# Full attention: small jobs on turned maxima and outputs moved from VectorE to ScalarE and GpSimd

## The reference

```python
def _L1_attn_ref(x, Wq, bq, Wk, bk, Wv, bv, Wo, bo):
    q = (x @ Wq.T + bq).reshape(b, s, NHEADS, DK)
    k = (x @ Wk.T + bk).reshape(b, s, NHEADS, DK)
    v = (x @ Wv.T + bv).reshape(b, s, NHEADS, DV)
    w = jnp.einsum('bshd,bzhd->bhsz', q, k)
    w = w / jnp.sqrt(jnp.float32(DV))
    w = jax.nn.softmax(w, axis=-1)
    vw = jnp.einsum('bhsz,bzhd->bshd', w, v)
    out = vw.reshape(b, s, NHEADS * DV) @ Wo.T + bo
    return out
```

## Time and profile before

| what | us |
|---|---|
| median of three runs (2055.39 to 2059.88) | 2056.86 |
| span of the profiled execution | 2056.4 |
| attention stage, first exponential to last division | 986.4 to 1637.7 |
| of it, first to last exponential, 256 steps | 986.4 to 1634.0 |
| busy in the whole span: PE / DVE / ACT / POOL | 1579.5 / 1339.0 / 1135.7 / 550.2 |

### The profile page before, as it was taken

One profiled execution on the slowest core, in us unless ns is written; L12 is line 12 of the kernel. 1 busy time (PEld: TensorE's weight loads), 2 busy tenths in 40 slices (PEclk: granted clock), 3 DMA queues, 4 the chain that ended last, 5 costly groups with the idle time before them and its releaser, 6 DMA issues. The chain is left out here.

```text
span 2056.4 us, 34421 instructions
## 1 busy us (share of the span) xinstructions
PE 1579.5 (77%) x11512; PEld 917.7 (45%) x11512; DVE 1339.0 (65%) x3318; ACT 1135.7 (55%) x2965; POOL 550.2 (27%) x615
## 2 busy tenths in 40 slices
PE   6799999999991699245999999999999735424910
PEld 3478777777771699221222222222222234323910
DVE  5655656656564322267999999999999287842523
ACT  3366766666651344142688888888888733111300
POOL 2133323524526400571001001001000020372056
PEclk9799999999995799666899999999999967556965
DMA  5144311211101676142000000000000000013832
GB/s 191 39 156 156 107 30 36 54 28 43 42 21 37 203 234 205 52 122 83 23 21 26 18 26 18 27 18 26 19 25 2 1 0 6 21 45 124 253 91 72
DMA packets 86203, 138.99 MB, mean 68 GB/s; under 512 B 18084, under 2 KB 57252, under 8 KB 85900
## 3 DMA queue, kind: packets, MB, share of 16 engines
q1 hardware_dynamic: 62860, 92.08, 15.2%
q0 software_dynamic: 11936, 34.49, 5.1%
q10 hardware_dynamic: 11232, 10.23, 1.4%
HBM read 75.51 MB, written 45.11 MB: 59 GB/s over the span
## 5 line engine op out<-in xcount | busy, mean ns | idle before, releaser
L2062 DVE TENSOR_REDUCE q_max<-s_ps 128x1 f32<-128x1024 f32 x512 | 598.2, 1219 | 14.0 <-PE s_ps L1953 6.8
L2043 ACT ACTIVATE probs<-s_ps 128x512 f32<-128x512 f32 x1024 | 535.5, 603 | 124.5 <-PE s_ps L1974 124.3
L1953 PE MATMUL s_ps<-k_stack,q_stack 64*128 64x512 bf16 x1024 | 351.2, 397 | 16.9 <-PEq L96 8.5
L1974 PE MATMUL s_ps<-q_stack,k_stack 64*128 64x512 bf16 x1024 | 319.5, 384 | 20.2 <-ACT probs L2043 15.8
L1988 PE MATMUL o_ps<-probs,v_aug 128*32 128x512 f32 x2048 | 273.6, 606 | 0.7 <-ACT probs L2043 0.7
L1974 PEld LDWEIGHTS s_ps<-q_stack,k_stack 64*128 64x128 bf16 x1024 | 78.6, 94 | 333.9 <-ACT probs L2043 281.9
L989 POOL TENSOR_TENSOR probs<-probs,p_rsum 128x512 f32<-128x512 f32 x128 | 132.9, 1038 | 325.8 <-DVE p_rsum L966 325.1
L869 ACT ACTIVATE probs<-s_biased,s_min 128x128 f32<-128x128 f32 (+1 forms) x512 | 197.7, 391 | 37.0 <-DVE s_min L960 35.6
L734 PE MATMUL score_ps<-k_pad,q_bd 128*128 128x128 f32 x1024 | 146.7, 287 | 0.0
L960 DVE CUSTOM_DVE_ANT_0 s_biased<-score_ps,nbias 128x128 f32<-128x128 f32 (+1 forms) x512 | 115.8, 282 | 41.8 <-PE score_ps L734 40.6
L1580 POOL CAST neg_max_parts<-neg_max 16x128 bf16<-16x128 f32 x32 | 9.0, 281 | 474.7 <-DVE neg_max L2070 474.7
(11 more groups left out here) (315 smaller groups left out, 2824.5 us busy)
## 6 DMA issues: line engine op xcount, KB each, us to landing
moe0b_wblock<-in_L_ffn_blocks SPq DMA_DIRECT2D x39, 578.0 KB, 3.9
moe_rows<-zero_rows POOLq DMA_DIRECT2D x18, 960.0 KB, 4.4
moe1b_wblock<-in_L_ffn_blocks SPq DMA_DIRECT2D x39, 256.0 KB, 3.5
v_shift<-v_tiles SPq DMA_DIRECT2D x32, 256.0 KB, 3.1
v_shift<-v_tiles SPq DMA_DIRECT2D x32, 224.0 KB, 3.6
qk_parts_dram<-qk_parts SPq DMA_DIRECT2D x16, 384.0 KB, 2.7
q_stack<-qk_parts_dram SPq DMA_DIRECT2D x192, 32.0 KB
k_stack<-qk_parts_dram SPq DMA_DIRECT2D x192, 32.0 KB
```

Of the source, the lines that this page charges most:

```text
L1953: mm = nc.tensor.matmul(s1[u % 2][:, c * CH:(c + 1) * CH], qs[head_rows(m), quad % 4, j, qt * P:(qt + 1) * P], ks[head_rows(m), quad % 4, ...
L1974: nc.tensor.matmul(bank_of("exp", 4 * k + pos)[:], ks[head_rows(m), quad % 4, j, kt * P:(kt + 1) * P], qs[head_rows(m), quad % 4, j, half ...
L2043: nc.scalar.activation(pr[:, k % 2, HEADS[pos], :], bank_of("exp", n)[:], ACT.Exp).then_inc(sm["exp"], 1)
L2062: v.tensor_reduce(mx[:, h % 4, col:col + 1], s1[u % 2][:], AX.X, ALU.max).then_inc(sm["maxed"], 1)
```

## The change

Three things are moved; TensorE's program keeps its order, and waits for the new release of a bank (`o_read` in place of `o_done`).

- The negation of the turned maxima goes from VectorE to ScalarE, as an activation Copy with scale -1.
- The turned outputs, 9 columns of 16 head and token groups, are copied by ScalarE from the bank into a new tile `o_tokens` in two buffers; that copy frees the bank.
- GpSimd divides from `o_tokens`: a power with the exponent -1 on the sums, then the product into `nat`. It sets a tile of -1 once ahead of the loop.

VectorE keeps the row maxima alone. ScalarE does the moved work of step k - 1 behind the first exponential of step k. The core of the diff:

```diff
             @block.gpsimd
+                def divide(m):
+                    pool.wait_ge(sm["o_read"], m + 1)
+                    if m >= 2:
+                        pool.wait_ge(sm["o_done"], m - 1)
+                    nc.gpsimd.tensor_tensor(ro[:, m % 2], ot[:, m % 2, :, :, HD1], minus[:], ALU.pow).then_inc(sm["o_rsum"], 1)
+                    pool.wait_ge(sm["o_rsum"], m + 1)
+                    nc.gpsimd.tensor_tensor(
+                        K.nat[:, t:t + CPT, s * 32:(s + 1) * 32].rearrange("p t (h d) -> p t h d", d=HD1),
+                        ot[:, m % 2, :, :, 0:HD1], bc(ro[:, m % 2], 3, HD1), ALU.mult
+                    ).then_inc(sm["o_done"], 1)
...
                 for quad in range(NQ):
                     if quad >= 2:
+                        divide(2 * quad - 3)
                         pool.wait_ge(sm["pv_mm"], STEPS * (quad - 1))
...
                     if quad >= 1:
                         split_max(2 * quad - 1)
+                        divide(2 * quad - 2)
                     split_max(2 * quad)
+                divide(2 * NQ - 3)
                 split_max(2 * NQ - 1)
+                divide(2 * NQ - 2)
+                divide(2 * NQ - 1)
...
             @block.scalar
+                def negate_max(h):
+                    act.wait_ge(sm["m_turned"], h + 1)
+                    if h >= 1:
+                        act.wait_ge(sm["m_split"], 4 * h)
+                    nc.scalar.activation(nm[:], turned_view(bank_of("m_neg", h))[0:HU, 0, :], ACT.Copy, scale=-1.0
+                                         ).then_inc(sm["m_neg"], 1)
+                def read_output(m):
+                    act.wait_ge(sm["o_turned"], m + 1)
+                    if m >= 2:
+                        act.wait_ge(sm["o_done"], m - 1)
+                    heads = turned_view(bank_of("o_read", m)).rearrange("p t (h c) -> p t h c", c=32)
+                    nc.scalar.copy(ot[:, m % 2], heads[:, :, :, 0:HD1 + 1]).then_inc(sm["o_read"], 1)
+                def behind_first(k):
+                    if max_done_at(k) is not None:
+                        negate_max(max_done_at(k))
+                    if output_due_at(k) is not None:
+                        read_output(output_due_at(k))
+                negate_max(0)
                 for k in range(NK):
                     for pos in range(4):
...
+                        if pos == 0 and k >= 1:
+                            behind_first(k - 1)
                         if pos == 2 and k % TPB == 0 and k >= TPB:
                             output(k // TPB - 1)
+                behind_first(NK - 1)
                 output(2 * NQ - 1)
+                read_output(2 * NQ - 1)
...
             @block.vector
-                    if u == HU:
-                        negate_max(0)
                 for k in range(NK):
                     for u in step_units(k):
                         reduce_max(u)
-                    if max_done_at(k) is not None:
-                        negate_max(max_done_at(k))
-                    if output_due_at(k) is not None:
-                        divide(output_due_at(k))
-                divide(2 * NQ - 1)
```

More of the change, by code:

```diff
@@ L1765 @@
             "m_stored", "m_loaded",
-            "s2_mm", "exp", "v_aug", "pv_mm", "o_out", "o_turned", "o_done", "o_rsum")
+            "s2_mm", "exp", "v_aug", "pv_mm", "o_out", "o_turned", "o_read", "o_rsum", "o_done",
+            "minus_set")
 def full_attention_stage(nc, K, A, wo, M):
@@ L1827, in full_attention_stage @@
         mp = K.sb("neg_max_parts", [2 * TPB, 2, 3, P], BF16, ctx=st)
+        ot = K.sb("o_tokens", [P, 2, CPT, 4, HD1 + 1], ctx=st)
         ro = K.sb("o_rsum", [P, 2, CPT, 4], ctx=st)
+        minus = K.sb("minus_one", [P, CPT, 4], ctx=st)
         s1 = [K.ps(f"s1_ps{i}", [P, T], st) for i in range(2)]
@@ L1873, in full_attention_stage @@
             if output_due_at(k) is not None:
-                uses.append(("o_done", output_due_at(k)))
-        uses.append(("o_done", 2 * NQ - 1))
+                uses.append(("o_read", output_due_at(k)))
+        uses.append(("o_read", 2 * NQ - 1))
         place = {use: r for r, use in enumerate(uses)}
@@ L1925, in split_max @@
                            nr[:])
+                def divide(m):
+                    quad, half = divmod(m, 2)
+                    b, s = divmod(quad, QUADS)
+                    t = b * TPB + half * CPT
+                    pool.wait_ge(sm["o_read"], m + 1)
[7 more added lines that the diff above has]
+                    ).then_inc(sm["o_done"], 1)
+                nc.gpsimd.memset(minus[:], -1.0).then_inc(sm["minus_set"], 1)
+                pool.wait_ge(sm["minus_set"], 1)
                 wo.gate(pool)
@@ L1994, in turn_output @@
                     pe.wait_ge(sm["o_out"], m + 1)
-                    wait_bank(pe, "o_done", m)
+                    wait_bank(pe, "o_read", m)
                     for t in range(CPT):
-                        x = nc.tensor.transpose(turned_view(bank_of("o_done", m))[:, t, :],
+                        x = nc.tensor.transpose(turned_view(bank_of("o_read", m))[:, t, :],
                                                 osb[:, m % 2, t * P:(t + 1) * P], K.ident[:])
```

## The result

The changed kernel takes 2088.41 us (median of four runs, 2086.49 to 2089.93), beside 2058.37 of the kernel before on the same chip: a ratio of 1.0147, 95% interval 1.0132 to 1.0161. That is 30 us slower (27 to 33). The profiled span is 2087.3 us, 30.9 more than before.

The account below looks back on a forecast made before the run. The prediction took a ring of score products, exponentials and v product over three banks as the bound, not VectorE. Its terms, 14.0 + 15.2 - 2.7 + 2.8 = 29.3 us, added to 2056.86 gave 2086, range 2079 to 2104.

Parts of the forecast that it names:

- The ring as the bound: Full attention: score products, exponentials and v product, waiting on three PSUM banks in turn, set the 2.39 us step, without VectorE.
- Usual steps: Full-attention steps without turned maxima or turned outputs; forecast to stay at 2.39 us.
- The negation: Turned maxima negated on ScalarE, freeing the bank later; 0.45 us each, 31 times in the loop, 14.0 us slower.
- The read-out: Turned outputs copied from their bank by ScalarE, freeing it 0.49 us later, 31 times in the loop; 15.2 us slower.
- E(k+1,0): First of ScalarE's four exponentials in step k+1; both moved jobs were forecast to stand behind it.
- VectorE relieved: Step behind the division no longer waits for late maxima: 0.09 us, 30 times, 2.7 us saved.
- The stage's end: Last division, now with GpSimd's power, which nothing hides behind the loop; 2.8 us more (1.9 to 3.6).
- (a): Rival: VectorE bounds the full attention, so the change makes it faster, 2026 us; chance 0.06.
- (b): Rival: ScalarE's two short jobs vanish in its idle 0.33 to 0.49 us a step; 2057, no change; chance 0.04.
- (c): Rival: GpSimd's power is far slower than expected and delays the maxima's split; at 10 us, 2134; chance 0.04.
- two special steps in eight: Steps where maxima are turned and negated (2.61 us) or outputs turned and divided (2.97); forecast 3.06 and 3.46 after.

Follow-up runs that it names:

- e_half_max: Kernel before the change, with row maxima over the first 512 of the 1024 keys; 2048.81 us in one run.
- e_pow_twice: Changed kernel with each GpSimd power taken twice; 2091.17 us, ratio 1.0161 to the kernel before.
- e_early_last: Changed kernel with ScalarE's two jobs ahead of the step's first exponential and the stage's last division on VectorE; 2052.84 us, ratio 0.9972 to the kernel before.
- e_read_back: Changed kernel with read-out and division given back to VectorE, only the negation on ScalarE; 2073.17 us, ratio 1.0083 to the kernel before.
- e_early: Changed kernel with ScalarE's two jobs put ahead of the step's first exponential; 2056.05 us, ratio 1.0001 to the kernel before.
- e_late: Changed kernel with ScalarE's two jobs put behind the step's second exponential; 2120.78 us, ratio 1.0314 to the kernel before.

## Why the prediction was right

The forecast was 2086 in a range of 2079 to 2104; the measured time is 2088.41, and the span grew by 30.9 where the sum said 29.3. The sum was added to 2056.86; the kernel before beside the result has 2058.37, which makes most of the 2.2 us between forecast and median. Point by point:

- **The ring as the bound.** Usual steps stayed at 2.39 in every kernel, with VectorE at full, less and half work. Shown by `e_half_max`, and before any run by the earlier trace rows. TensorE's load as such isn't the bound either: in the stretch of the earlier trace rows the first pass is over, TensorE is busy 13.27 of 16 us, and the steps are as long.
- **The negation**, 0.45 forecast: the step grew from 2.61 to 3.07, 0.46. The job takes 249 ns at 263 forecast. The estimate after the Trainium skill ("ScalarE: Activation LUTs", "What ACT_TABLE_LOAD costs"), 293 ns, was too long; here the line through the copies of the earlier trace rows was nearer.
- **The read-out**, 0.49 forecast: from 2.97 to 3.47, 0.50; it takes 273 ns at 275 forecast. Both start 0.49 behind E(k+1,0), as read from the earlier trace rows.
- **VectorE relieved**, 0.09 forecast for each step behind a division: 2.48 became 2.40. The three terms of the loop together: 26.5 forecast, 27.3 measured.
- **The stage's end**, 2.8 forecast, 3.6 measured: this is the term that was mis-sized. The power takes 2.90 at the 2.5 that I chose between 1.7 and 3.3; and from the last product's end to the next stage's first weights pass 1.68 (1668.13 to 1669.81), where VectorE's product was followed after 1.20. The sum put this second part at nothing. It doesn't go by the engine that ends the stage: behind GpSimd's product it is 1.25 in `e_pow_twice`, behind VectorE's 1.51 in `e_early_last` and 1.23 in `e_read_back`. What sets it stays open.
- **Rivals.** (a), VectorE as the bound, is refuted for the kernel before, but for 0.08 us in eight steps; it becomes true for one step in eight once the bank is in time. The Trainium skill, "Perfetto Trace Analysis", section "Identifying the Most-Contended Engine", has one optimize the engine of highest occupancy first. Here that would have misled: VectorE, busy 155.06 of 162 us, was not what the steps waited for. (b) fell with `e_early` and `e_late`: ScalarE's idle time hides the jobs only ahead of E(k+1,0). (c) fell with the power at 2.90 and with `e_pow_twice`.

One thing the prediction overlooked, without harm to the sum. It counts two special steps in eight, and there is a third: the first step of a half, where ScalarE's copy of the sums stands behind E(k,2). In the kernel before, such a step starts at 1310.70 and the next at 1313.29:

```profile
1312.81 0.59 ACT L2035 COPY o_sb<-o_ps 128x512 f32<-128x512 f32 x1
1313.29 2.07 ACT L2043 ACTIVATE probs<-s_ps 128x512 f32<-128x512 f32 x4
```

It takes 2.59 in every kernel and so drops out of the differences. But rival (a), which lets all eight steps fall to 2.39, could have gained 0.90 in eight steps at most, not 1.10.

## What to carry to other kernels

When a few buffers turn round among several users, a small job that frees one is priced by the moment at which it frees it: by what stands ahead of it in its engine's order more than by its own length, and not by how busy that engine is. Before taking work off the busiest engine, look for a stretch where that engine has nothing to do: if the steps are as long there, it is not the bound. And when the first bound is loosened, expect the next one close behind: here it took back 0.26 of the 0.39 us that the early jobs should have gained in eight steps.

## What the hardware showed that I had not expected

GpSimd's power took 1.65 us for 128 x 8 elements and 2.90 for 128 x 16: by these two shapes 0.16 us a column and some 0.4 besides, so neither a fixed price nor quite one per column (the exponent was -0.5 in the first and -1 in the second). And ScalarE starts the next exponential 0.16 after a short copy has started (1309.66 to 1309.82), though the copy's own row lasts 0.27; behind an exponential, whose row lasts 0.60, the copy itself starts after 0.49 (1309.17 to 1309.66). In both cases the next instruction starts 0.11 before the row ahead of it ends, and for the short job that is two fifths of its row.
